# Three small moves in a float32 attention layer: one write ahead of two weight loads, the first square roots ahead of a weight split, a scaling into the last group

## What is computed

```python
x = L0_attn_q
xn = _layernorm(x, axis=-1)
s = _L0_attn_ref(xn, w_qkv, w_dense)      # 8 groups x 4 heads, causal softmax, then @ w_dense.T
g = _silu(_L0_ffn_ref(xn, k0, s0, k1, s1, k2, s2))
x = x + s * g

# inside the network: a scale and a factor of 2 around each hidden layer
h = s0 * conn_dense(k0, x)
h = jax.nn.relu(h) * 2.0
```

## Time and profile before

| | us |
|---|---|
| median of three runs | 907.86 |
| lowest and highest | 906.57 and 910.95 |
| the profiled execution | 912.13 |
| its span on the core | 909.8 |
| PE busy | 896.5 (99%) |
| DVE, ACT, POOL busy | 669.7, 519.6, 466.3 |

### The profile page before, as it was taken

The page is one execution under the profiler, slowest core; times in us unless marked ns, Lnnn a source line. Parts: engine busy times, 40 slices in busy tenths (PEclk is TensorE's granted clock), DMA queues, the critical chain, the costliest instruction groups (busy, mean ns, idle before and its releaser), DMA issues.

```text
span 909.8 us, 16000 instructions
## 1 busy us (share of the span) xinstructions
PE 896.5 (99%) x4297; PEld 758.9 (83%) x4297; DVE 669.7 (74%) x1162; ACT 519.6 (57%) x1096; POOL 466.3 (51%) x372
## 2 busy tenths in 40 slices
PE   7999999999999999999999999999999999999998
PEld 6878888888888888888888888888888888888886
DVE  6778766778678766888667776787667786677756
ACT  3656645665365645666456644656456563585552
POOL 4345653565355634556336634546545563346666
PEclk9999999999999999999999999999999999999999
DMA  5687655866487764765577674776548565556464
GB/s 185 180 216 207 139 106 151 236 157 140 80 214 210 166 119 112 233 180 117 112 183 213 161 149 83 200 221 147 115 117 265 139 134 97 150 143 148 105 137 153
DMA packets 204980, 143.83 MB, mean 158 GB/s; under 512 B 23168, under 2 KB 172416, under 8 KB 204928
## 3 DMA queue, kind: packets, MB, share of 16 engines
q1 hardware_dynamic: 176256, 129.68, 56.8%
q10 hardware_dynamic: 28672, 13.64, 6.8%
HBM read 63.70 MB, written 23.20 MB: 96 GB/s over the span
## 4 chain that ended last, share of the span: by engine, by line
issue 49%; POOL 32%; PE 16%; DVE 1%; POOLq 1%; ACT 0%; DMA 0%; SPq 0%; DVEq 0%
POOL pt_lo L788 24%; POOL w_lo L800 5%; POOL wd_lo L800 3%; PE ps_m L1324 3%; PE ps_m L1163 2%; PE ps_m L1165 2%; PE ps_m L1164 2%; PE ps_s L1309 2%; PE ps_o L1163 1%; PE ps_o L1164 1%; PE ps_o L1165 1%; PE ps_s L1164 1%; PE ps_s L1165 1%; PE ps_s L1163 1%; DMA raw<-wqkv 0%
## 5 line engine op out<-in xcount | busy, mean ns | idle before, releaser
L788 POOL TENSOR_TENSOR pt_lo<-pt_lo,pt_hi 128x512 fp32r<-128x512 f32 x248 | 328.3, 1349 | 285.0 <-ACT pt_hi L910 284.9
L1007 DVE CUSTOM_DVE_ANT_0 ps_s<-ps_s,mask 128x32 f32<-128x32 f32 (+31 forms) x256 | 182.3, 714 | 115.3 <-PE ps_s L1165 114.1
L910 ACT ACTIVATE pt_hi<-pt_lo 128x512 fp32r<-128x512 f32 x288 | 169.4, 625 | 52.9 <-PE ps_o L1165 35.5
L1163 PE MATMUL ps_m<-xn_hi,w_hi 128*128 128x512 f32 (+1 forms) x392 | 153.5, 392 | 2.6 <-DVE k_lo L1107 1.9
L1165 PE MATMUL ps_m<-xn_hi,w_lo 128*128 128x512 f32 (+1 forms) x392 | 151.9, 387 | 0.0
L1164 PE MATMUL ps_m<-xn_lo,w_hi 128*128 128x512 f32 (+1 forms) x392 | 151.8, 387 | 0.0
L1165 PE MATMUL ps_s<-k_hi,q_lo 128*128 128x480 f32 (+15 forms) x384 | 126.6, 330 | 0.0
L1164 PE MATMUL ps_s<-k_lo,q_hi 128*128 128x480 f32 (+15 forms) x384 | 126.6, 330 | 0.0
L1163 PE MATMUL ps_s<-k_hi,q_hi 128*128 128x480 f32 (+15 forms) x384 | 124.9, 325 | 0.4 <-ACT prob_odd L854 0.4
L854 ACT ACTIVATE prob_odd<-ps_s,small 128x160 f32<-128x160 f32 (+15 forms) x128 | 96.1, 753 | 44.2 <-DVE small L1007 37.3
L854 ACT ACTIVATE prob_even<-ps_s,small 128x32 f32<-128x32 f32 (+15 forms) x128 | 82.5, 645 | 63.0 <-DVE small L1007 61.1
(11 more groups left out here) (105 smaller groups left out, 1459.1 us busy)
## 6 DMA issues: line engine op xcount, KB each, us to landing
raw<-wqkv SPq DMA_DIRECT2D x48, 256.0 KB, 3.3
pt_lo<-prob_odd SPq DMA_DIRECT2D x96, 128.0 KB, 3.7
pt_lo<-prob_even SPq DMA_DIRECT2D x96, 112.0 KB, 3.3
pt_lo<-prob_odd SPq DMA_DIRECT2D x96, 96.0 KB, 2.6
raw<-wd SPq DMA_DIRECT2D x32, 256.0 KB, 6.0
inv_rows<-inv SPq DMA_DIRECT2D x32, 256.0 KB, 3.9
at_lo<-inv SPq DMA_DIRECT2D x32, 256.0 KB, 3.6
turned<-prob_odd SPq DMA_DIRECT2D x32, 256.0 KB, 4.0
```

The lines of the kernel that those rows point to most:

```text
L788: pool.tensor_tensor(pt_lo[:, slot, :], pt_lo[:, slot, :].bitcast(F32), pt_hi[:, hi_slot, :], ALU.subtract).then_inc(land_lo, 1)
L910: act.activation(pt_hi[:, hi_slot, :], pt_lo[:, LAND_AT[i] + j, :].bitcast(F32), ACT.Copy).then_inc(land_hi, 1)
L1007: dve.tensor_tensor_reduce(out=scores, in0=scores, in1=mask[:, S - width(i % BLOCKS, tile):S], scale=-1.0, scalar=BIG, op0=ALU.add, op1=AL ...
L1163: pe.matmul(out, sta_hi, mov_hi, start=start, stop=False)
```

## The change

Three moves in the tables. In the body `dw.1` and `rw.1` move up behind `load.q1`, so that the loads of q2 and q3 stand behind them. In the prologue `root.0` moves ahead of `hi.split.q0` on ACT. `ffn_scales` moves from the end of DVE's prologue to the beginning of DVE's last group.

```diff
-    act = [("root_table",)] + hi(split[0]) + root[:1] + hi(*ln(0, 1), split[1]) + root[1:2] + hi(*ln(2, 3), split[2], units[0]) \
+    act = [("root_table",)] + root[:1] + hi(split[0], *ln(0, 1), split[1]) + root[1:2] + hi(*ln(2, 3), split[2], units[0]) \
...
-    dve += [("ffn_scales",)]
...
     "sp": """
-        load.q0 load.q1 load.q2 load.q3 dw.1 rw.1 load.k load.v dr.1 rr.1 dw.2 rw.2 dw.3 rw.3 dr.2
+        load.q0 load.q1 dw.1 rw.1 load.q2 load.q3 load.k load.v dr.1 rr.1 dw.2 rw.2 dw.3 rw.3 dr.2
...
     "dve": """
-        max.1.0 max.1.1 max.1.2 max.1.3 max.2.0 flip.1 lo.unit.q3.1 max.2.1 inverse.1 max.2.2
+        ffn_scales max.1.0 max.1.1 max.1.2 max.1.3 max.2.0 flip.1 lo.unit.q3.1 max.2.1 inverse.1 max.2.2
```

## The result

The two kernels were timed side by side in three sessions (medians in us):

| | before | changed | ratio, 95% interval |
|---|---|---|---|
| first | 909.89 (20 runs) | 906.57 (20) | 0.9967, 0.9960 to 0.9974 |
| second | 908.33 (29) | 907.08 (11) | 0.9984, 0.9975 to 0.9993 |
| third | 908.44 (22) | 906.45 (11) | 0.9976, 0.9967 to 0.9985 |

What follows compares the result with a forecast made beforehand. PE was taken to set the pace, with gains only where it pauses: prologue, seam to the loop, group 0. Forecast: 907.86 - 1.1 - 0.5 - 2.4 = 903.9 us, own range 902.5 to 905.2, 8-in-10 range 902.0 to 906.4.

Steps and rivals of the forecast that it cites:

- the starting level: Median of the kernel before, taken as 907.86 us from three runs that spread over 4.4 us.
- All three terms: Gains subtracted from 907.86 us: first roots 1.1, doubled scales 0.5, row block 1's write 2.4 us.
- the pause: Group 0: PE waits 1.85 us, until 53.41, behind exp.3.0; with the slow clock after it, 3.8 us.
- The sum for the profiled execution: Whole kernel, profiled execution: 1.1 + 0.5 + 3.8 = 5.4 us gained, from 912.13 to 906.7.
- The write: Group 0: row block 1's writes land earlier, so PE's pause and slow clock go; 2.4 us of the median.
- The landing of the last write: Group 0: issued at 42.6, lands 5.4 us later at 48.0, with 512 KB less ahead; bounds 45.3 and 49.6.
- The roots: Prologue: first root on ACT at about 5.70 instead of 6.83, 1.1 us gained, bounds 0.8 and 1.13.
- The scales: Prologue's end: DVE's 1.10 us operation seems to wait for POOL; moving it gains PE 0.5 us, bounds 0 and 0.6.
- The rival of the loop's entry: Loop start: the 1.10 us belongs to entering the loop, not POOL; 0.5 us less gain, 904.4; chance 0.12.
- The warning about the slowest DMA engine: Group 0: one slow engine holds the writes, so the pause stays; only 1.6 us won, 906.3; chance 0.15.
- The slower rival: Groups 1 to 6: late q2 and q3 loads delay row block 1's read, 1.7 us each; 914; chance 0.04.

## Why the prediction was wrong, point by point

**Two steps failed: the starting level and the size of the gain.** 903.9 was 907.86 less 4.0. Over 20 runs the kernel before has a median of 909.89, 2.0 us higher. The same 4.0 us from there give 905.9, inside the range; measured is 906.57. The text took three runs as the level and gave the range no term for their spread. In the first session the level is 2.0 us of the miss of 2.7 and the gain (3.3 for 4.0) is 0.7. That share is luck, since 3.3 is the largest gain of the three sessions. In the second the level (908.33) accounts for 0.5 us and the gain of 1.3 for 2.7; in the third it is 0.6 and 2.0.

**All three terms were too large.** In median spans the single moves gave 1.4 us (write, 2.4 in the sum), 0.5 (roots, 1.1) and 0.0 (scales, 0.5), together 1.9. The whole change gave 1.9 and 1.95. So in spans the moves add up; in times they gave 1.3, 0.2 and -0.5. That one move takes back what another gains is thus argued from the pause, and the medians do not need it. The intervals of the single moves reach 0.8 to 1.0 us to either side, so this agreement is closer than the runs can guarantee. The range of the forecast was also drawn too narrow at its top: with the lower bound of each term (0.8, 0 and 1.3) its own sum is 905.8 and not 905.2.

**The sum for the profiled execution held.** It named 5.4 us and 5.7 were measured, with group 0 at 105.31 us where 105.3 to 105.8 had been named. The 906.7 us that it gave for the changed kernel is 0.1 off the measured 906.57; the way from there to 903.9 was the mistake. But the earlier trace rows show an extreme execution. Its span of 909.8 lies above all 103 spans of that kernel on record, of the session that followed (35 spans, 905.6 to 908.9, median 907.0) and the later ones (highest 909.5). The text saw this danger and discounted the pause from 3.8 to 2.4 us. The write alone brought 1.3, the lower bound that it had given. A likely part of the reason is that the slow clock, about 1.5 us of the 3.8, belongs to few executions.

**The write: mechanism right, size off.** The pause that the rows show went, and the clock stayed at 2.4 GHz with it. That `exp.3.0` would start by 47.4 held (45.73). That the cause is the landing of the write, as said, is borne out by PE's wait being gone in all nine profiles with the write behind q1 or q0 and being there in all six with it behind q3 or k. The landing of the last write was estimated at 5.4 us after its issue, from 512 KB less in the queue; it took 3.4, the shortest of the eight profiles with this order:

```profile
turned<-prob_odd SPq DMA_DIRECT2D x1, 128.0 KB, 3.4
```

The reckoning by bytes came out about right on average, 1.4 us for 1.6, though single executions scatter by 2 us. Besides, moving the write issues it 1.1 us earlier in the group.

**The roots: 1.1 us was the best case and stood as the value.** The prediction named what is late next, the load of x block 3, which it found 0.07 us late, and charged 0.1 us. Block 2, which DVE needs first, was as near and not reckoned. Loads of another execution come 1 us later: `x` block 2 took 4.6 us there and 5.6 in the changed kernel's profile, block 3 took 4.9 and 5.8. DVE then waited 0.98 us, and in five of six later profiles with the roots ahead and the same loads 0.18 to 0.45. The gain depends as much on how late q0's weights are. With the roots behind the split they start at 5.92 to 7.17 us in five profiles, ahead of it at 5.42 to 5.66. The move measured 0.2 us alone and 0.6 beside the moved write, in spans 0.5 and 0.8.

**The scales: the cause right, the gain too small to see.** The operation waited for POOL: 1.10 us beside its subtraction in all four profiles where it stands ahead of the loop, 0.16 us where POOL rests, in two places. The Trainium skill ("SBUF — State Buffer", "SBUF: two separate sides") has this as its lock rule, for DVE operations in a two-port mode or with two inputs in SBUF, and these rows agree with it. Not every small operation waits, as the kernel before shows while POOL subtracts:

```profile
10.98 1.28 POOL L800 TENSOR_TENSOR w_lo<-raw,w_hi 128x512 fp32r<-128x512 f32 x1 [0.54 <-ACT w_hi L952]
11.44 0.15 DVE L981 RECIPROCAL vt<-vt 128x2 f32<-128x2 f32 x1
11.63 0.65 DVE L984 TENSOR_TENSOR vt<-vt 128x2 f32<-128x2 f32 x1
```

The reciprocal is through in 0.15 us in the middle of POOL's subtraction. The operation behind it, on numbers of the same size, ends at 12.28 as POOL does at 12.26. The rival of the loop's entry is refuted. PE's wait of 0.40 us went, too. In the median it did not show: the 0.5 us is within what the pause of group 0 takes back or the runs scatter.

**The warning about the slowest DMA engine** was weighed as a rival at 0.15 and as a stay of the pause. It did not come true in that form: in no profile with the write behind q1 or q0 did PE wait for it. In a weaker form it was right, since from one execution to the next the time to landing varied by 2 us with the same bytes ahead.

**The slower rival** did not happen. Groups 1 to 6 take 630.4 us together, against 631.2 before. But its kind, a load held back behind the write, is what cost 9 us when q0 was held back as well. The prediction had looked up the first use of q2 and q3, and for them its reckoning held.

## What to carry to other kernels

Before a forecast stands on a pause that a single profile shows, ask whether that execution is typical: hold its span against those of the other runs, and if only three times are known, give the level itself a term in the range. A step that is moved out from behind a wait is worth its time only if the resource behind it is ready; a margin under the scatter of a load's landing (here about 1 us) is no margin. When a transfer is moved up, check the first use of every load that it is moved past: behind q0 it gained, ahead of q0 it lost 9 us.

## What was not expected of the hardware

- The granted clock of PE fell after waits of 1.85 and 1.94 us (granted clock 0.71 and 0.59 over 52 to 56 us) and stayed at 1.00 in that window after one of 1.58 us.
- A DVE operation on 128x3 numbers took 1.10 us beside POOL's subtraction and 0.16 us otherwise, while a reciprocal on 128x2 numbers took 0.15 us beside one.
- The last write of row block 1, 128 KB, landed 5.0 to 7.0 us after its issue in group 0 behind four loads and 3.4 to 5.4 us behind two. In group 1 it took 2.3 or 2.4 us in all ten profiles with two loads or fewer ahead, and 2.5 to 4.1 us in the other six.
- The part of a time that lies outside the span is 2.2 us in most executions, and up to 3.9 in some of the kernel before and up to 4.0 in some of the changed one. It widens the scatter of times beyond that of the spans.
